# Four packed values per bucket, the source count inside the histogram, one-hots in quads, and a build without products of zeros

## The reference, cut to what matters

```python
# L0: two hops of  x = 0.5 * D^-1/2 (A + I) D^-1/2 x + 0.5 * h ; relu; two dense layers
# L1: hypergraph:  he = segment_sum(x'[src], dst, 2500); out = segment_sum(he[dst], src); @ W.T + b
# L2: out = (x + 3 * segment_sum(edge_weight * x[dst], src)) / 4
# L3: softmax over all edges of relu(attr @ Wh + [x[src], x[dst]] @ Wn) @ w_e, scattered by src
for layer in (L0, L1, L2, L3):
    x = layernorm(x + layer(x))
```

## Time and profile before

| what | value |
|---|---|
| three runs | 7845.85, 7877.51, 7887.17 us; median 7877.51 us |
| the profiled execution | 7873.77 us, its span 7872.0 us |
| TensorE busy (products; weight loads) | 3812.2 us (48%); 2422.8 us (31%) |
| VectorE, ScalarE, GpSimd busy | 3389.4 us (43%); 1127.3 us (14%); 3603.0 us (46%) |
| granted TensorE clock, mean | 0.76 of full speed |
| HBM read, written | 502.61 MB, 144.27 MB |

### The profile page before, as it was taken

One profiled execution on the slowest core, in us unless ns is written; L12 is line 12 of the kernel. 1 busy time (PEld: TensorE's weight loads), 2 busy tenths in 40 slices (PEclk: granted clock), 3 DMA queues, 4 the chain that ended last, 5 costly groups with the idle time before them and its releaser, 6 DMA issues. The chain is left out here.

```text
span 7872.0 us, 98123 instructions
## 1 busy us (share of the span) xinstructions
PE 3812.2 (48%) x16163; PEld 2422.8 (31%) x16164; DVE 3389.4 (43%) x11703; ACT 1127.3 (14%) x3853; POOL 3603.0 (46%) x3613
## 2 busy tenths in 40 slices
PE   1600150016666775775945554333333356666665
PEld 0300030001111342443423332232322256665663
DVE  4946370026666444114021113333333555665666
ACT  0000000001111000002000001000000244444443
POOL 0045777710000684660056664666666155555550
PEclk9999999987777896887955555555555578888886
DMA  9411111261111563652711111111111233333332
GB/s 129 72 30 36 48 42 53 53 23 78 75 78 73 202 210 106 220 168 87 274 43 45 45 45 42 45 44 43 44 44 44 48 95 95 95 98 95 95 98 35
DMA packets 674873, 648.60 MB, mean 82 GB/s; under 512 B 495848, under 2 KB 564441, under 8 KB 655638
## 3 DMA queue, kind: packets, MB, share of 16 engines
q1 hardware_dynamic: 546182, 379.55, 18.1%
q0 software_dynamic: 128384, 266.34, 12.2%
q10 hardware_dynamic: 144, 1.28, 0.0%
HBM read 502.61 MB, written 144.27 MB: 82 GB/s over the span
## 5 line engine op out<-in xcount | busy, mean ns | idle before, releaser
L828 POOL DMA_INDIRECT bucketed_edges<-edge_rows,idx x784 | 817.6, 1043 | 784.0 <-issue 725.3
L483 POOL DMA_INDIRECT gathered<-node_table,idx x576 | 624.4, 1084 | 1130.7 <-ACT idx L471 958.4
L1337 POOL DMA_INDIRECT gathered<-node_table_xq,idx x832 | 796.3, 957 | 752.8 <-issue 223.7
L359 POOL DMA_INDIRECT gathered<-node_table,idx x816 | 772.7, 947 | 495.9 <-issue 249.8
L374 PE MATMUL ps<-onehots,gathered 128*128 128x128 f32 x1632 | 430.6, 443 | 846.7 <-DVE agg L402 609.0
L663 POOL DMA_INDIRECT gathered<-node_table,idx x588 | 556.1, 946 | 330.7 <-issue 171.7
L430 PE MATMUL ps<-gathered,junk 128*128 128x512 f32 x1182 | 622.4, 636 | 125.7 <-DMA gathered<-edge_counts 125.6
L678 PE MATMUL ps<-onehots,gathered 128*128 128x128 f32 x1176 | 467.7, 501 | 409.3 <-DMA gathered<-node_table,idx 394.9
L374 PEld LDWEIGHTS ps<-onehots,gathered 128*128 128x128 f32 x1632 | 365.1, 327 | 912.2 <-issue 834.3
L1177 PE MATMUL ps<-onehots 128*128 128x512 bf16 x1152 | 472.4, 487 | 187.0 <-DVE onehots L1204 183.9
L678 PEld LDWEIGHTS ps<-onehots,gathered 128*128 128x128 f32 x1176 | 294.6, 311 | 582.4 <-DMA gathered<-node_table,idx 559.4
(11 more groups left out here) (373 smaller groups left out, 6729.2 us busy)
## 6 DMA issues: line engine op xcount, KB each, us to landing
gathered<-edge_counts SPq DMA_DIRECT2D x99, 1280.0 KB
edge_counts<-gathered SPq DMA_DIRECT2D x49, 1280.0 KB
gathered<-node_table,idx POOLq DMA_INDIRECT x1980
bucketed_edges<-edge_rows SPq DMA_DIRECT2D x52, 544.0 KB, 12.5
edge_rows<-bucketed_edges SPq DMA_DIRECT2D x208, 128.0 KB
gathered<-edge_counts SPq DMA_DIRECT2D x48, 512.0 KB
side_rows<-edge_counts SPq DMA_DIRECT2D x48, 512.0 KB
edge_rows<-in_edge_attr_dram SPq DMA_DIRECT2D x108, 128.0 KB
```

The source lines that it names most:

```text
L359: nc.gpsimd.indirect_dma_start(g[:, k, :], None, table, bass.IndirectOffsetOnAxis(m.idx[:, k:k + 1], 0)).then_inc(S["landed"][k], 16)
L483: nc.gpsimd.indirect_dma_start(g[:, k, :], None, a.table, bass.IndirectOffsetOnAxis(m.idx[:, k:k + 1], 0)).then_inc(S["landed"][k], 16)
L828: nc.gpsimd.indirect_dma_start(a.bucketed, bass.IndirectOffsetOnAxis(m.idx[:, k:k + 1], 0), m.erow[:, k, :], None).then_inc(S["scattered"] ...
L1337: nc.gpsimd.indirect_dma_start(g[:, k, :], None, a.table2, bass.IndirectOffsetOnAxis(m.idx[:, k:k + 1], 0)).then_inc(S["landed"][s], 16)
```

## The change: what it does

- **prepare:** the instruction that counts a bucket moves into the loop of the histogram, in front of each step's one-hots; its wait comes at the end of the step.
- **lists:** the table has four integers for each bucket: for each range the first tile plus 1024 times the number of pairs, and the number of pairs before the bucket. Seven small operations for each range take the place of two, and of three over the whole table. Each of the three ranges has at least two pairs now.
- **build:** the registers hold 4 values; shifts, masks and sums on the sequencers give the three numbers of each range, and one check for each bucket takes the place of three. TensorE waits for the range's banks and lets the range's first product open them; the first pair stands ahead of a loop from 1 to n. The products of zeros are gone.
- **light:** the one-hots of a quad are one comparison of 512 columns (`iota` from PSUM), a wait for it, and one multiplication in place by the four weights.

```diff
@@ -45,6 +45,9 @@
 KW = NK * KB
 PARTS = ((0, 1), (1, 3), (3, 5))
 NR = len(PARTS)
+ROWL = NR + 1
+LO = 1024
+assert BT < LO
 WB = KB * max(b - a for a, b in PARTS)
 SPLIT = (E - (P - 1) * NT) // U
 DUMP = BT * P
@@ -272,12 +275,9 @@
             step(V.memset(m.hwrow[:, M:KW], 0.0))
             step(V.memset(m.side[:, NP:AW], 0.0))
 
-            with v.Fori(0, NB) as i:
+            with v.Fori(0, NI) as i:
                 b = bass.ds(i, 1)
                 V.tensor_scalar(m.tabs[:, 0:NT], m.shi, m.iota[:, b], None, ALU.is_equal, ALU.add, accum_out=m.cnt[:, b]).then_inc(S["counted"], 1)
-                v.wait_ge(S["counted"], i + 1)
-
-            with v.Fori(0, NI) as i:
                 for h in range(2):
 
                     v.wait_ge(S["hist_used"], i * 2 + h + 1)
@@ -288,6 +288,7 @@
                     for k in range(HALF):
                         V.tensor_scalar(m.ohlo[:, h * HALF + k, :], m.iotab[:, :], m.dlo[:, bass.ds(i * U + h * HALF + k, 1)],
                                         None, ALU.is_equal).then_inc(S["hist_ready"], 1)
+                v.wait_ge(S["counted"], i + 1)
             v.wait_ge(S["hist_used"], 2 * NI + 3)
             V.tensor_scalar(m.deg[:, :], m.ps[:, 7, 0:NB], 1.0, None, ALU.add).then_inc(S["degree"], 1)
             v.wait_ge(S["root"], 1)
@@ -336,7 +337,7 @@
 
     off, NQ = m.off, U // G
     g = m.gather[:, 0:U * D].rearrange("p (t d) -> p t d", d=D)
-    with phase(nc, name, f"landed*{U} idx_ready used onehot added dve") as (S, block):
+    with phase(nc, name, f"landed*{U} idx_ready used onehot equal added dve") as (S, block):
 
         def loop(eng, body):
             with eng.Fori(0, eng.value_load(iters, min_val=1, max_val=BT // U)) as n:
@@ -382,20 +383,23 @@
             v.sem_inc(S["added"], U)
             step(V.tensor_copy(m.startI[0:1, :], m.start[0:1, :]))
 
-            def onehots(t0, q):
-
-                for e in range(G):
-                    k = bass.ds(t0 + G * q + e, 1)
-                    last = V.tensor_scalar(m.oh[:, G * q + e, :], m.iota[:, :], off[:, k], weight[:, k], ALU.is_equal, ALU.mult)
-                last.then_inc(S["onehot"], 1)
+            step(V.tensor_copy(m.ps[:, 7, 512 - P:512], m.iota[:, :]))
+            four = lambda cols: cols.unsqueeze(2).to_broadcast([P, G, P])
+
+            def onehots(t0, q, made):
+
+                oh, k = m.oh[:, G * q:G * q + G, :], bass.ds(t0 + G * q, G)
+                V.tensor_tensor(oh, m.ps[:, 7, 512 - P:512].unsqueeze(1).to_broadcast([P, G, P]), four(off[:, k]), ALU.is_equal).then_inc(S["equal"], 1)
+                v.wait_ge(S["equal"], made + 1)
+                V.tensor_tensor(oh, oh, four(weight[:, k]), ALU.mult).then_inc(S["onehot"], 1)
             for q in range(NQ):
-                onehots(0, q)
+                onehots(0, q, q)
 
             def body(t0, n):
                 start = window_starts(nc, mybir.EngineType.DVE, m, t0, U)
                 for q in range(NQ):
                     v.wait_ge(S["used"], n * NQ + q + 1 + NQ)
-                    onehots(t0 + U, q)
+                    onehots(t0 + U, q, n * NQ + q + NQ)
                     for e in range(G):
                         v.wait_ge(S["added"], t0 + G * q + e + U)
                         w = m.agg[:, bass.ds(start[G * q + e], WIN)]
@@ -1043,8 +1047,8 @@
     inb, rev, fwd, f = (m.gather[0:NB, k * BT:(k + 1) * BT] for k in range(4))
     one, two = m.gather[:, 4 * BT:5 * BT], m.gather[:, 5 * BT:6 * BT]
     first, past = m.lists[PB, 0:NR + 1], m.lists[PB, 6:7 + NR]
-    rowF = m.gather[0:1, 6 * BT:6 * BT + 3 * NB * NR]
-    three = rowF.rearrange("p (b k c) -> p b k c", k=NR, c=3)
+    rows = m.gather[0:1, 6 * BT:6 * BT + 2 * NR * NB].rearrange("p (c b) -> p c b", b=NB)
+    rowsI = m.gather[0:1, 6 * BT + 2 * NR * NB:6 * BT + 3 * NR * NB].bitcast(I32).rearrange("p (c b) -> p c b", b=NB)
     pairs, ends = (m.gather[0:1, 7 * BT + j * NB * NR:7 * BT + (j + 1) * NB * NR] for j in range(2))
     halves = lambda t: t.rearrange("p (h t) -> p h t", h=2)
     with phase(nc, "lists", "dve cmp marked counted taken listed rows") as (S, block):
@@ -1075,18 +1079,23 @@
             step(V.tensor_scalar(first, first, -1.0, float(BT), ALU.mult, ALU.add))
             step(V.tensor_scalar(first, first, float(BT - 1), None, ALU.min))
             step(V.tensor_tensor(past, past, first, ALU.subtract))
-            V.tensor_scalar(past, past, 1.0, None, ALU.max).then_inc(S["listed"], 1)
+            step(V.tensor_scalar(past[:, 0:NR], past[:, 0:NR], 3.0, None, ALU.max))
+            V.tensor_scalar(past[:, NR:NR + 1], past[:, NR:NR + 1], 1.0, None, ALU.max).then_inc(S["listed"], 1)
             v.wait_ge(S["rows"], 2 * NR)
+            table = m.startI[0:1, 0:ROWL * NB].rearrange("p (b c) -> p b c", c=ROWL)
+            by_bucket = lambda t: t.rearrange("p (b k) -> p b k", k=NR)
             for q in range(NR):
-                step(V.tensor_copy(three[:, :, q, 0], m.ps[0:1, 5, q * NB:(q + 1) * NB]))
-                step(V.tensor_scalar(three[:, :, q, 1], m.ps[0:1, 5, (NR + q) * NB:(NR + q + 1) * NB], 1.0, None, ALU.add))
-            step(V.tensor_copy(m.startI[0:1, 0:3 * NB * NR], rowF))
-            step(V.tensor_scalar(m.startI[0:1, 0:3 * NB * NR].rearrange("p (i c) -> p i c", c=3)[:, :, 1],
-                                 m.startI[0:1, 0:3 * NB * NR].rearrange("p (i c) -> p i c", c=3)[:, :, 1], 1, None, ALU.arith_shift_right))
-            step(V.tensor_copy(pairs, m.startI[0:1, 0:3 * NB * NR].rearrange("p (i c) -> p i c", c=3)[:, :, 1]))
+                first_tile, n = rows[:, q, :], rows[:, NR + q, :]
+                step(V.tensor_copy(first_tile, m.ps[0:1, 5, q * NB:(q + 1) * NB]))
+                step(V.tensor_scalar(n, m.ps[0:1, 5, (NR + q) * NB:(NR + q + 1) * NB], 1.0, None, ALU.add))
+                step(V.tensor_copy(rowsI[:, q, :], n))
+                step(V.tensor_scalar(rowsI[:, q, :], rowsI[:, q, :], 1, None, ALU.arith_shift_right))
+                step(V.tensor_copy(by_bucket(pairs)[:, :, q], rowsI[:, q, :]))
+                step(V.scalar_tensor_tensor(first_tile, by_bucket(pairs)[:, :, q], float(LO), first_tile, ALU.mult, ALU.add))
+                step(V.tensor_copy(table[:, :, q], first_tile))
             step(V.tensor_tensor_scan(ends, m.ones[0:1, 0:1].to_broadcast([1, NB * NR]), pairs, 0.0, ALU.mult, ALU.add))
             step(V.tensor_tensor(ends, ends, pairs, ALU.subtract))
-            step(V.tensor_copy(m.startI[0:1, 0:3 * NB * NR].rearrange("p (i c) -> p i c", c=3)[:, :, 2], ends))
+            step(V.tensor_copy(table[:, :, NR], by_bucket(ends)[:, :, 0]))
 
         @block.tensor
         def _(pe):
@@ -1115,7 +1124,6 @@
     ohs = [low[:, 2 * WB + e * P:2 * WB + (e + 1) * P] for e in range(2)]
     iotaI = m.hid[:, :, :].rearrange("p t d -> p (t d)").bitcast(I32)[:, 0:WB]
     iotaK = m.junk[:, :, :].rearrange("p t d -> p (t d)").bitcast(FP16)[:, 0:WB]
-    zeros = m.zerob[:, 0:1].to_broadcast([P, KB])
     with phase(nc, "build", "iota dve ready used summed emptied stored*2") as (S, block):
 
         def walk(eng, body):
@@ -1127,12 +1135,13 @@
 
         def lists(eng, engine, b):
 
-            got = nc.values_load_multi_w_load_instructions(m.startI[0:1, bass.ds(b * (3 * NR), 3 * NR)], engines=[engine])[1]
-            return [got[3 * k:3 * k + 3] for k in range(NR)]
-
-        def bounded(eng, before):
-
-            return eng.snap(nc.s_assert_within(before, 0, NK * (BT + NB)))
+            got = nc.values_load_multi_w_load_instructions(m.startI[0:1, bass.ds(b * ROWL, ROWL)], engines=[engine])[1]
+            before, at = eng.snap(nc.s_assert_within(got[NR], 0, NK * (BT + NB))), []
+            for k in range(NR):
+                n = eng.snap((got[k] >> 10) & 511)
+                at.append((eng.snap(got[k] & (LO - 1)), n, before))
+                before = eng.snap(before + n)
+            return at
 
         @block.sync
         def _(sp):
@@ -1165,17 +1174,19 @@
             def body(b, e, u):
                 at = lists(pe, mybir.EngineType.PE, b)
                 for r, (k0, k1) in enumerate(PARTS):
-                    for k in range(k0, k1):
-                        pe.wait_ge(S["emptied"], b * NK + k + 1)
-                        T.matmul(m.ps[:, k, :], m.zerob[:, :], zeros, start=True, stop=False)
-                    n, before = at[r][1], bounded(pe, at[r][2])
-                    with pe.Fori(0, n) as j:
-                        c = pe.snap((before + j) * 2)
+                    n, before = at[r][1], at[r][2]
+
+                    def pair(c, first):
                         for h in range(2):
                             pe.wait_ge(S["ready"], c + (h + 1))
                             for k in range(k0, k1):
-                                last = T.matmul(m.ps[:, k, :], ohs[h], ohd[h][:, (k - k0) * KB:(k - k0 + 1) * KB], start=False, stop=False)
+                                last = T.matmul(m.ps[:, k, :], ohs[h], ohd[h][:, (k - k0) * KB:(k - k0 + 1) * KB],
```

(9 more changed lines are left out.)

## The result

The changed kernel took 7967.31 us (median of four runs, 7951.42 to 7988.01) where the kernel before took 7872.84 (four runs, 7845.85 to 7887.17): a ratio of 1.0126 as estimated from the runs (the two medians divided give 1.0120), 95% interval 1.0088 to 1.0163. It is slower by 1.3%, and the forecast of 7753 us was wrong in size and in sign.

A forecast was written before the change was run, and what follows sets the result against it. VectorE and its sequencer were taken to set the pace in build and light. Histogram -22, lists +3, build registers -83 and light -19 summed to -121 us, from 7873.77 profiled to 7753; 8-in-10 range 7690 to 7815 us.

The forecast's parts named there:

- Build, arithmetic: Build: fewer checks offset the added shifts, masks and sums, about as many register operations; 0, with 25 us either side.
- Build, registers: Build: loading four aligned values takes 0.352 us where nine took 2.075; 83 us saved over all buckets.
- R4: Rival, build: register loads slow by their place between pipelined work, not by count; saving only 30, 7806 us; chance 0.11.
- Build, zeros and two pairs: Build: dropping products of zeros taken as 0 (at most -45 us); at least two pairs per range 0 to +5, taken 0.
- Histogram and lists: Prepare: moving the count hides its wait, -22 us (-24 to -10); lists: more small steps, +3 us (+2 to +6).
- Light: Light: fewer VectorE instructions bring gathers to members' pace, -36 us, against multiplication's +17; sum -19 us (-60 to +80).
- The other sign: Light: a sign of the forecast being right, that TensorE would hardly wait for the additions any more.
- The multiplication's price: Light: multiplying two SBUF operands on VectorE delays the gathers, taken as 17 us between attend's 7 and hop1's 97.
- R3: Rival, slower: light's chain is work, not instructions, and gathers also lose time; light +199 us, total 7971; chance 0.04.
- The chance of 0.03 for slower: Whole kernel: the forecast's chance of a time slower by over 0.5% (39 us), beside 0.93 for faster and 0.04 within.

The follow-up runs named there:

- e11_masks_in_before: Kernel before with masks that change nothing and pairs ahead summed on the engines, nine values and zeros kept: 8155.23 us in one profiled run, build 1050.6.
- e8_kept: Changed kernel with each unpacked value moved once per bucket into its own register, with checked bounds, on VectorE and TensorE: 8038.36 us, ratio 1.013, build 958.9 us.
- e12_kept_cheap: Changed kernel with unpacked values kept in registers on both engines, without runtime bound checks on them: 7806.15 us, ratio 0.9899, build 836.0 us.
- e3_zeros_back: Changed kernel with the products of zeros and TensorE's plain loop put back: 7990.78 us, ratio 1.0126, build 984.1 us.
- e13_padded12: Kernel before with its table padded to twelve integers per bucket: 6995.37 us in one profiled run, beside 7055.4 on that chip; build 794.4 us.
- e6_padded: Kernel before with its table padded to sixteen integers per bucket: 7834.16 us in one profiled run, build 794.1 us.

## Why the prediction was wrong

**Build, arithmetic: the step that failed.** The prediction put it as "shift, mask and sum for three ranges are added, about as many register operations. I take 0", with 25 us on either side. It priced them once for each bucket. The counts show them at each use: 3057 more register operations on VectorE, not 441. At 0.04 to 0.07 us each and some 0.03 to the next (in the trace after an operation of 0.04 us starts at 2104.30 and the next at 2104.37) an estimate is 250 us on the sequencer; a part of it hides below VectorE's own instructions, and the pairs grew by 166 us and more. e11_masks_in_before adds the arithmetic to the kernel before and loses 199 us; e8_kept and e12_kept_cheap take it out of the loops of the changed kernel and the pairs are short again. The bound should have come from the same sentence as in light, where it was said that the sequencer's instructions set the pace: the one-hots of 722 tiles were about to be reached through expressions instead of registers, and an expression's price is its length times its uses.

**Build, registers: right in kind, mis-sized.** The load fell to 0.354 us as foreseen. But "2.075 us ... on 48 buckets" took a median for all, and the minimum, 0.862, was not that of bucket 0 (1.104 us): 12 of the 48 later loads took 0.87 us, so the mean was 1.76 and the saving 1.40 x 49 = 69 us, not 83. The pauses gave 59 of them (from 2.74 to 1.51 us in the mean; 2.91 was one bucket's). R4 thought of the load's place among pipelined work. What the runs show is its place in the table: that is worth 1.2 us of the 1.7, the count the other 0.5. R4 did not come about: four values at a multiple of 16 bytes are both few and well placed.

**Build, zeros and two pairs: right.** 0 and 7 us, from both sides; both kernels have 361 pairs.

**Histogram and lists: right.** -26.6 for -22, +2.5 for +3. Prepare gained 5 us more than the wait of 21.6; where they come from stays open.

**Light: right in sum, in part by its mechanism.** -22.3 for -19. Waits after, in the stretch that answers to the earlier trace rows, and the gathers' stretch that answers to the earlier trace rows:

```profile
PE ps L375 <- DVE agg L406: 448.6, 142, 15.1
...
DVE agg L406 <- issue: 324.3, 354, 3.2
...
DVE onehots L392 <- issue: 160.9, 75, 7.4
...
DVE onehots L394 <- issue: 59.6, 95, 2.7
```

```profile
5069.00:6219.00 1150.00, 761.24 (x785) 0.50 0.17 45
```

The idle time before one-hots fell from 355.0 to 220.5 us (forecast 150), some of it moved to the additions (275.3 to 324.3), and a gather comes each 1150 / 785 = 1.465 us, inside the 1.45 to 1.48 that was to show it right. The other sign did not come: TensorE was hardly to wait for the additions any more, and it still waits 448.6 us (583.9 before). So the pace of members (1.449 us) was nearly reached, but not because the additions stopped being late. The multiplication's price was forecast as 17 us of longer gathers: they take 761.24 / 785 = 0.970 us instead of 0.946, 20 us over 816. It is the multiplication: over the whole phase, the 236 gathers that overlap one take 1.026 us in the mean, the other 580 take 0.946, and all of the 55 that last over 1.05 us overlap a multiplication and none a comparison. The Trainium skill (SBUF - State Buffer, "SBUF: two separate sides") spoke against this part: by its rule a VectorE instruction with two SBUF inputs and a GpSimd instruction that reads SBUF lock each other out for the whole instruction, so each multiplication could hold GpSimd for its whole length. The traces agree that there is a loss, but 20 us over 208 multiplications are 0.1 us each, not 0.69.

**The rivals.** None of the four was the case. R3 had the sign and its number, 7971, was within 4 us of the result, but that is luck: its mechanism, a loss in light, did not happen. The chance of 0.03 for slower left out that the arithmetic, the term with the least evidence, could lie far on the other side.

## What to carry to other kernels

Before arithmetic on registers is priced, find out where it is evaluated: count the sequencer's instructions by line and divide by the number of turns of the loops around them. Where a sequencer sets the pace, move a derived value into a register of its own once, and leave out its checked assertion where the bound is known otherwise. And before a table is made smaller, see whether its rows only start in the wrong place: padding shortened the pauses by 43 us where packing shortened them by 59, for 0.8 us of lists and no arithmetic.

## What the runs showed of the hardware

- A register load of nine integers by VectorE takes 0.86 us from a multiple of 16 bytes in the table and 2.08 us from the starts between (4, 8 and 12 bytes past one); of four, from a multiple of 16 bytes, 0.35 us. The first load of the phase is longer, 1.10 us for nine and 0.60 for four. The period of four buckets in the kernel before (36 bytes each) and the table of 48 bytes both fit that; a multiple of 64 is not needed.
- On VectorE's sequencer a register operation with a checked bound takes 0.228 us in e8_kept, a plain one there 0.045, and nine checked ones for each bucket lengthened the pause from 2.46 us (e12_kept_cheap) to 4.99.
- The clock's record of the build reads 1.00 in the changed kernel, while its products last 606 to 634 ns, as long as the one of the earlier trace rows at 2115.23. In e3_zeros_back, with the same length of the build, it reads 0.61. The mean of the whole execution is recorded as 0.794 in two runs of the changed kernel and as 0.732 in the two others, at the same time within 0.5%: 0.062 x 7972 = 494 us, half the length of the build. A record of 1.00 should be held against the duration of a product.
- One chip was much faster in the phases with gathers: where e13_padded12 ran, the kernel before took 7055.4 us (one run); attend lasted 1106.7 us there and light 1033.0, where e6_padded had 1456.5 and 1234.3. The build was the same to 0.3 us.
